# Second attention of a four-part layer chain: one order of units through all batches, values issued ahead of transposes, and the transposed probabilities drained by VectorE alone

## What is computed

```python
qp = q @ Wq.T
kv = latent_kv @ Wkv_expand.T
k, v = jnp.split(kv, 2, axis=-1)
...
scores = jnp.einsum('bhqd,bhkd->bhqk', qh, kh) * inv_sqrt_d
scores = jnp.where(causal, scores, jnp.finfo(scores.dtype).min)
attn = jax.nn.softmax(scores, axis=-1)
out = jnp.einsum('bhqk,bhkd->bhqd', attn, vh)
out = out.transpose(0, 2, 1, 3).reshape(b, sq, H)
return out @ Wout.T
```

## Time and profile before

| | |
|---|---|
| median of 3 runs | 1895.05 us (1893.91 to 1896.69) |
| the profiled execution | 1879.77 us, span 1877.9 us, mean granted clock 0.941 |
| busy share of the span | PE 89%, PEld 71%, DVE 72%, ACT 54%, POOL 50% |
| the second attention | 1479.9 us (first scores) to 1707.3 us (last addition) |
| maxima, L1925 | x49, 1225 ns each |
| exponentials, L1882 | x264, 106.8 us in all |
| drains on VectorE, L1933 | x32 at 686 ns, x16 at 1221 ns |
| drains on ScalarE, L1891 | x32 at 621 ns |
| key masks on GpSimd, L1741 | x18, 1895 ns each |

### The profile page before, as it was taken

How to read it: one execution, slowest core, us unless ns; L and a number is a source line. 1 busy time by engine, 2 the same in 40 slices (tenths; PEclk the granted TensorE clock), 3 DMA queues, 4 the chain that set the end, 5 groups by cost and what they waited for, 6 DMA issues and landing times. The chain is left out here.

```text
span 1877.9 us, 48860 instructions
## 1 busy us (share of the span) xinstructions
PE 1674.9 (89%) x16216; PEld 1332.3 (71%) x16216; DVE 1353.5 (72%) x2952; ACT 1010.8 (54%) x2015; POOL 942.2 (50%) x625
## 2 busy tenths in 40 slices
PE   7437999999999999999999999979777777876998
PEld 5235888888888888888888888868656344445876
DVE  6876888888888888888888888866555355654323
ACT  5133666666666676666666676641212356653211
POOL 3703777777777777777777777740002111111311
PEclk8567999999999999999999999989888899996999
DMA  9421112122122122121121141158100000004234
GB/s 272 144 65 58 51 57 83 49 61 78 49 69 70 49 78 62 49 85 54 49 91 49 53 139 62 55 160 262 58 1 21 20 13 12 10 7 164 88 116 155
DMA packets 150137, 144.13 MB, mean 77 GB/s; under 512 B 41290, under 2 KB 137208, under 8 KB 149584
## 3 DMA queue, kind: packets, MB, share of 16 engines
q1 hardware_dynamic: 144144, 135.33, 23.8%
q10 hardware_dynamic: 4416, 4.29, 0.7%
q0 software_dynamic: 1536, 3.99, 0.6%
HBM read 92.01 MB, written 33.98 MB: 67 GB/s over the span
## 5 line engine op out<-in xcount | busy, mean ns | idle before, releaser
L1059 POOL TENSOR_TENSOR c_rest<-c_prob 128x1024 f16<-128x1024 f32 (+1 forms) x513 | 796.8, 1575 | 314.4 <-ACT c_prob L902 301.8
L978 DVE TENSOR_REDUCE c_mxp<-c_psM 128x1 f32<-128x400 f32 (+1 forms) x1040 | 589.2, 573 | 114.3 <-PE c_psM L762 99.8
L902 ACT ACTIVATE c_prob<-c_psS,ln,c_exp_scale 128x1024 f32<-128x1024 f32 (+1 forms) x514 | 536.7, 1044 | 243.4 <-PE c_psS L778 238.2
L778 PE MATMUL c_psS<-c_q,c_kk 128*128 128x256 f16 (+1 forms) x3350 | 512.7, 272 | 1.7 <-ACT c_prob L902 1.6
L796 PE MATMUL c_psV<-c_vb,c_prob 128*128 128x129 f16 (+1 forms) x3328 | 396.5, 222 | 0.5 <-POOL c_rest L1059 0.5
L778 PEld LDWEIGHTS c_psS<-c_q,c_kk 128*128 128x128 f16 (+1 forms) x3350 | 321.7, 99 | 87.7 <-ACT c_prob L902 2.2
L799 PE MATMUL c_psV<-c_vb,c_rest 128*128 128x65 f16 (+1 forms) x3328 | 374.0, 193 | 0.0
L762 PE MATMUL c_psM<-c_kkm,c_q 128*128 128x400 f16 (+1 forms) x1040 | 348.2, 335 | 5.8 <-DVE c_mxp L978 3.6
L799 PEld LDWEIGHTS c_psV<-c_vb,c_rest 128*128 128x128 f16 (+1 forms) x3328 | 301.4, 99 | 22.1
L796 PEld LDWEIGHTS c_psV<-c_vb,c_prob 128*128 128x128 bf16 (+1 forms) x3328 | 305.2, 97 | 14.7 <-POOL c_rest L1059 0.7
L724 PE MATMUL c_psQ<-c_xb,c_w2s 128*128 128x256 f16 x1188 | 163.7, 275 | 4.2 <-DVE c_roped L946 2.5
(11 more groups left out here) (295 smaller groups left out, 2176.8 us busy)
## 6 DMA issues: line engine op xcount, KB each, us to landing
c_w2s<-w_scr SPq DMA_DIRECT2D x67, 256.0 KB, 2.6
acc_scr<-c_acc SPq DMA_DIRECT2D x128, 129.0 KB, 2.1
c_ms<-m_scr SPq DMA_DIRECT2D x67, 192.0 KB, 2.3
c_w2s<-w_scr SPq DMA_DIRECT2D x67, 128.0 KB, 2.0
kv<-acc_scr SPq DMA_DIRECT2D x4, 2064.0 KB, 9.9
d_acc<-acc_scr SPq DMA_DIRECT2D x4, 2064.0 KB, 8.2
m_w<-in_L_ffn_W SPq DMA_DIRECT2D x16, 352.0 KB
c_vb<-V SPq DMA_DIRECT2D x27, 129.0 KB, 2.0
```

The costliest lines, as they stand in the source:

```text
L778: mm = pe.matmul(psS[g % 2][0:r, i * S:(i + 1) * S], src[:, (lo + i) * P:(lo + i) * P + r], mov[slot][:, :], start=(one == 0 and i % 2 == ...
L902: nc.scalar.activation(prob[g][0:r, 0:w], psS[g % 2][0:r, 0:w], ACT.Exp, bias=keep["ln1024"][0:r, :], scale=exp_scale[slot][0:r, :]).then_ ...
L978: nc.vector.tensor_reduce(mxp[:, st, c:c + 1], psM[:, st, 0:CHUNKS[c][1]], AX.X, ALU.max).then_inc(mx_done, 1)
L1059: nc.gpsimd.tensor_tensor(rest[g][0:r, 0:w], prob[g][0:r, 0:w], high[0:r, 0:w], ALU.subtract).then_inc(rest_done, 1)
```

## The change

The units run through the batch boundaries in one order, on every engine. On TensorE the step becomes: scores of the next unit, values of the unit before, transposes of this unit; what stood behind a batch's six steps (values of unit 5, second reciprocals) moves into the next batch's step 0, and `project` moves from step 0 to step 2. On ScalarE the drains are gone (`pt_act` with them), `copy_r` moves ahead of the exponentials of its step, and the loop takes the same shape as on the other engines. On VectorE `drain_t` always copies 1024 columns and goes to the end of the step; `add` moves from step 0 to step 2, and the second `reciprocals` from behind the batch to step 5, ahead of that step's drain.

```diff
--- before.py
+++ after.py
@@ -1687,7 +1687,7 @@
     bias_ready = sem("bias_ready")
     exp_done = sem("exp_done")
     t_full = sem("t_full")
-    pt_done, pt_act = sem("pt_done"), sem("pt_act")
+    pt_done = sem("pt_done")
     pv_done = sem("pv_done")
     r_chain, r_ready, r_full = sem("r_chain"), sem("r_ready"), sem("r_full")
     r_copied = sem("r_copied")
@@ -1698,8 +1698,6 @@
 
     HALF_H = NH // 2
     KINDS = [((0, 1, 2, 3), P, 0), ((0, 2), S, 1), ((1, 3), S, 1)]
-    ACT_COLS = 512
-    ACT_DRAINS = (0, 1, 2, 2, 3, 4)
 
     def unit(k):
 
@@ -1785,10 +1783,6 @@
                 n = UNITS * b + k
                 pe.wait_ge(exp_done, n + 2)
                 pe.wait_ge(pt_done, n + 1)
-                if k == 0:
-                    pe.wait_ge(pt_act, 4 * b)
-                elif ACT_DRAINS[k - 1] > ACT_DRAINS[k - 2] or k == 1:
-                    pe.wait_ge(pt_act, 4 * b + ACT_DRAINS[k - 1])
                 for i in range(8):
                     mm = pe.transpose(psT[:, i * P:(i + 1) * P], prob[k % 2][:, i * P:(i + 1) * P], ident[:])
                 mm.then_inc(t_full, 1)
@@ -1799,8 +1793,6 @@
                 hh = k // 3
                 n = UNITS * b + k
                 pe.wait_ge(pt_done, n + 2)
-                if k % 3 != 0:
-                    pe.wait_ge(pt_act, 4 * b + ACT_DRAINS[k])
                 if k % 3 == 0:
                     pe.wait_ge(o_done, HH * b + hh + 1)
                     if hh == 0:
@@ -1852,21 +1844,24 @@
                         scores(b, k + 1, u)
                     else:
                         scores(b + 1, 0, 1 - u)
-                    transposes(b, k)
                     if k == 0 and not first:
+                        values(b - 1, UNITS - 1, 1 - u)
+                        reciprocals(b - 1, 1)
+                    elif k > 0:
+                        values(b, k - 1, u)
+                    if k == 2 and not first:
                         project(b - 1)
-                    if k >= 1:
-                        values(b, k - 1, u)
                     if k == 3:
                         reciprocals(b, 0)
-                values(b, UNITS - 1, u)
-                reciprocals(b, 1)
+                    transposes(b, k)
 
             batch(0, 0, first=True)
             with pe.Fori(0, B // 2 - 1) as j:
                 batch(2 * j + 1, 1)
                 batch(2 * j + 2, 0)
             batch(B - 1, 1)
+            values(B - 1, UNITS - 1, 1)
+            reciprocals(B - 1, 1)
             project(B - 1)
 
         @block.scalar
@@ -1884,13 +1879,6 @@
                                                accum_out=sums[:, hh, st * NH + h:st * NH + h + 1])
                 ins.then_inc(exp_done, 1)
 
-            def drain_t(b, k):
-                n = UNITS * b + k
-                act.wait_ge(t_full, n + 2)
-                act.wait_ge(pv_done, n + 1)
-                nc.scalar.activation(pT[k % 2][:, 1024 - ACT_COLS:], psT[:, 1024 - ACT_COLS:],
-                                     ACT.Copy).then_inc(pt_act, 1)
-
             def copy_r(b, hh):
                 n = HH * b + hh
                 act.wait_ge(r_full, n + 1)
@@ -1900,19 +1888,24 @@
             act.sem_inc(exp_done, 1)
             act.sem_inc(r_copied, 1)
             exps(0, 0)
-            with act.Fori(0, B // 2) as j:
-                for u in range(2):
-                    b = 2 * j + u
-                    for k in range(UNITS):
-                        if k < UNITS - 1:
-                            exps(b, k + 1)
-                        else:
-                            exps(b + 1, 0)
-                        if k % 3 != 0:
-                            drain_t(b, k)
-                        if k == 3:
-                            copy_r(b, 0)
-                    copy_r(b, 1)
+
+            def batch(b, first=False):
+                for k in range(UNITS):
+                    if k == 0 and not first:
+                        copy_r(b - 1, 1)
+                    if k == 3:
+                        copy_r(b, 0)
+                    if k < UNITS - 1:
+                        exps(b, k + 1)
+                    else:
+                        exps(b + 1, 0)
+
+            batch(0, first=True)
+            with act.Fori(0, B // 2 - 1) as j:
+                batch(2 * j + 1)
+                batch(2 * j + 2)
+            batch(B - 1)
+            copy_r(B - 1, 1)
 
         @block.vector
         def _(dve):
@@ -1929,8 +1922,7 @@
                 n = UNITS * b + k
                 dve.wait_ge(t_full, n + 2)
                 dve.wait_ge(pv_done, n + 1)
-                cols = 1024 if k % 3 == 0 else 1024 - ACT_COLS
-                nc.vector.tensor_copy(pT[k % 2][:, 0:cols], psT[:, 0:cols]).then_inc(pt_done, 1)
+                nc.vector.tensor_copy(pT[k % 2][:], psT[:]).then_inc(pt_done, 1)
 
             def reciprocals(b, hh):
                 n = HH * b + hh
@@ -1967,14 +1959,15 @@
                         maxima(b + 1, 0)
                     if k == 0 and not first:
                         normalise(b - 1, 1)
-                    drain_t(b, k)
-                    if k == 0 and not first:
-                        add(b - 1)
                     if k == 2:
                         reciprocals(b, 0)
+                        if not first:
+                            add(b - 1)
                     if k == 3:
                         normalise(b, 0)
-                reciprocals(b, 1)
+                    if k == 5:
+                        reciprocals(b, 1)
+                    drain_t(b, k)
 
             batch(0, 0, first=True)
             with dve.Fori(0, B // 2 - 1) as j:
```

## The result

| | before | after |
|---|---|---|
| median of 4 runs each | 1895.87 us (1893.91 to 1896.99) | 1844.81 us (1837.07 to 1848.15) |
| ratio, 95% interval | | 0.9728 [0.9706, 0.975] |
| the profiled execution, its span | 1879.77, 1877.9 us | 1842.96, 1841.1 us |
| first transposes to last addition | 219.46 us | 172.40 us (1487.38 to 1659.78) |
| stages behind it, to the end | 170.1 us | 180.2 us |

The change makes the kernel 51 us faster; 46 were predicted, and 1849 us. In the profiled executions the stage is 47.1 us shorter. The stages behind it are counted from the barrier, 1.1 us after the last addition begins. The same kernel timed again later (last experiment) gave 1832.86 against 1882.72, 49.9 us.

The account below looks back on a forecast made before the run. Waits going round between engines, mainly TensorE's on ScalarE's half drains, were taken as the bound. The stage was to fall from 219.5 to 173.0 us; 46 of the 46.5 saved, off 1895.05, gave 1849 us, range 1841 to 1862.

Parts of the forecast that it names:

- The sum: Stage from first transposes to last addition: first batch 20.0, six batches 129.0, last 24.0, in all 173.0 us.
- The chain of one batch: TensorE's order from T0 (transposes of unit 0) through V0 (its values) to the next batch's T0: 21.5 us.
- (1): ScalarE's four drains of 0.62 us a batch go; VectorE's four half drains grow from 0.69 to 1.23 us.
- (2): TensorE's step, values first: no new wait, transposes delayed by 0.57 us each, and 0.37 in steps 0 and 3.
- (3): Batch boundary: unit 5's values no longer precede the next second scores; the 2.35 us wait and low clock go.
- (4): TensorE's step 2: `project` costs 1.93 us ahead of transposes 2; the `add` that follows costs nothing.
- (5): ScalarE: `copy_r` ahead of the exponentials delays them 0.4 us twice a batch, covered by some 2 us of lead.
- (6): VectorE: second `reciprocals` ahead of drain 5 wait for one GpSimd mask; the drain starts 2.2 us after the maxima.
- Rival A: GpSimd keeps the reciprocals' copy out for both key masks: some 12 us more in all, 1861 us; chance 0.08.
- B: TensorE's clock still falls at boundaries, 1.6 us each, 13 us with the stage's end: 1862 us; chance 0.05.
- C: TensorE stays at 1.2 GHz through the stage: 29 us slower than before, 1924 us; chance 0.03.
- D: A wait read as ScalarE's has another source; the batch stays near 27 us, the program at 1895; chance 0.03.

Follow-up runs that it names:

- last experiment: The changed kernel itself, unaltered, profiled and timed again beside the kernel before on the same chip: 1832.86 against 1882.72 us, ratio 0.9733, stage 172.4 us.
- the kernel with the made gap: The change, with the first transposes of each batch also waiting for the exponentials of unit 1: stage 195.5 us, batches of 24.0 us.

## Why the prediction was right, point by point

**The sum** held: 173.0 for the stage, read 172.4, and again 172.4 in the last experiment. The first batch was 20.0, read 19.95 (1487.38 to 1507.33); six batches 129.0 together, read 128.65 (to 1635.98); the last 24.0, read 23.80. The chain of one batch, piece by piece, from the timeline between 1528.96 and 1550.35:

| piece | predicted | read |
|---|---|---|
| T0 to V0 | 2.41 | 2.58 |
| V0 to projection | 3.62 | 3.77 |
| projection to T2 | 1.93 | 1.83 |
| T2 to T3 | 3.35 | 3.20 |
| T3 to V3 | 2.41 | 2.43 |
| V3 to scores of the next unit 0 | 1.64 | 1.60 |
| those to V5 | 5.19 | 5.13 |
| V5 to T0 | 0.94 | 0.85 |

**(1) ScalarE's drains**: the reason given, its queue, was right. In the new order they are worth 16.2 us, in the old one 19.8, with the low clock in both numbers; by batches, 1.7 and 1.5 us each. VectorE was to be busy 17.9 us a batch, and is 17.4.

**(2) Values ahead of transposes** is where the argument failed, though the sum did not. The text has the swap only as a delay: "it delays each transposes by 0.57 us". Undone alone, it costs 28.6 us. The chain was laid out only for the order of the change, never for the one without the swap; the other order waits for exponentials 22 times. So the sum was right for the whole, and would have been no guide for a reader who wanted to leave that part out.

**(3) The boundary**: the 2.35 us wait and the low clock behind it went, as said. But the moves at the boundary are worth 29.5 us only where the values stand ahead (201.9 against 172.4), and nothing without (199.7 against 201.0). The low clock's share of before's loss is 8.5 us.

**(4), (5)** cost nothing that shows: the projection in step 2 took its 1.83 us.

**(6) The port**: 2.2 us from maxima to drain 5, read 2.12; copies of 0.8 to 0.9, read 0.78 to 0.85. Rival A is out. The wait at unit 5's values was to be about 1 us and is 0.5, because TensorE's own steps are longer than laid out: in sum it is busy for 20.8 us a batch, not 20.1. The term that was too small is the scores. They were priced ahead of transposes and by the starts of weight loads, 1.19 us; ahead of values they take 1.38 at least (1.60 for eight heads, not 1.41), and the 1.00 for transposes, not 1.07, gives back only a part. That this did not lengthen the batch is luck in part: most of it fell where TensorE would else have waited.

**B** did not happen, but the reason against it was too sure. "Each time the gap was over 2 us, while gaps of 1.2 us" did nothing: with 1.32 us and another 0.62 right behind, the clock fell at two of seven boundaries, and with 0.74 and 0.89 at one. **C**: the clock never stayed low, in any of these kernels. Its price leaves out the transposes, which at the low clock take 1.84 us (VectorE's drains alone, batch 0) in place of 1.04 to 1.10, six times a batch; C would have cost over twice the 29 us that it was given. "TensorE: Matmul & The Clock Gate" of the Trainium skill (A second HAM failure mode) has short idles swing the clock; before's boundaries and the kernel with the made gap agree with it, the change with idles of 0.5 us does not show it. **D** is out.

**The range** held, though its lower end does not follow from the terms given: 1844 less 0.5 and less 3 x 0.2 us in eight batches is about 1839, not 1841.

**From the stage to the total**: 46 us were taken off the median, 51 and 49.9 were measured, with an interval of 4 to 5 us on either side. The stage explains 47.1. The rest may be the stall, which is longer than the difference and lies in some executions and not in others, or falls of the clock that the timed runs of before have more often than the profiled one, or chance; the timed runs have no trace, so it stays open. The profiled execution was put at 1834 us and came to 1842.96, 10 of it the stall; the other one, without a stall, took 1832.86. The cause of the stall stays open too.

## What to carry to other kernels

Cost a reordering by laying out the whole ring once with and once without each part: here two of three parts are worth nothing alone and 27 us together. Where engines take turns, look at what stands in front of a drain in its queue before you look at busy shares, and put work that is ready ahead of the operation that waits. Once one engine is at 97%, moves on the others only exchange one small wait for another.

## What was not expected of the hardware

TensorE's granted clock fell behind idle gaps in this way, in seven boundaries and one execution each: 2.75 us six times, 2.48 three, 2.35 four, 1.32 with 0.62 right behind twice, 0.74 with 0.89 right behind once; with single waits of 1.42 inside the batch, 1.19 at the boundary and less, never (the stage's end apart, where the last projection was slow in several kernels). So a gap makes the fall likely and not certain, and a fall costs 0.7 to 2.0 us here, 1.6 in before. Twelve idle transposes in the gap took all of them away.

VectorE's copy of 128x256 takes 0.29 us alone. Begun within the first of two GpSimd operations of 1.9 us it takes 0.78 to 0.85 us and ends 0.14 us behind the end of that one; begun within the second it takes 1.03 to 1.39 and ends 0.13 to 0.15 us behind the end of the pair. GpSimd's pair, 3.74 us without a copy beside it, grows only to 3.79: VectorE is let in when an operation of GpSimd ends.

The stages behind the attention take some 10 us more in some executions and not in others of the same kernel: in the change's profiled execution two ScalarE operations began 4.5 and 9.2 us late, TensorE waited for them, and GpSimd went on. In a program of 1840 us that is more than many changes are worth.
